# Layer 1's attention: how far ahead the maximum pass runs

## The reference

```
Q, K, V = x @ W_Q.T, x @ W_K.T, x @ W_V.T        # split into 16 heads of 8
attn  = einsum('bhqd,bhkd->bhqk', Q, K) / sqrt(8)
attn  = where(tril(ones((1024, 1024))), attn, -inf)
probs = softmax(attn, axis=-1)
y     = einsum('bhqk,bhkd->bhqd', probs, V)
return y @ W_O.T
```

## Time and profile before

| what | us |
|---|---|
| median of three runs (1268.46 to 1277.15) | 1268.52 |
| profiled execution | 1278.86 |
| its span | 1276.6 |
| TensorE busy | 1111.2 (87%) |
| VectorE busy | 801.0 (63%) |
| ScalarE busy | 647.2 (51%) |
| GpSimd busy | 193.5 (15%) |
| mean granted clock of TensorE, share of full speed | 0.900 |

### The profile page before, as it was taken

How to read it: one execution, slowest core, us unless ns; L and a number is a source line. 1 busy time by engine, 2 the same in 40 slices (tenths; PEclk the granted TensorE clock), 3 DMA queues, 4 the chain that set the end, 5 groups by cost and what they waited for, 6 DMA issues and landing times.

```text
span 1276.6 us, 19532 instructions
## 1 busy us (share of the span) xinstructions
PE 1111.2 (87%) x7306; PEld 521.5 (41%) x7306; DVE 801.0 (63%) x1582; ACT 647.2 (51%) x1246; POOL 193.5 (15%) x312
## 2 busy tenths in 40 slices
PE   6499999699999999999854799899999899897777
PEld 4366666222222222222222344344442567553344
DVE  6633333498898899887047687788870435455654
ACT  4323322137787777778524156567775322424344
POOL 2145554000011010010100001112321000001000
PEclk9799999759999999999877589889995699899888
DMA  4612223311112101100004302211223300000331
GB/s 122 205 48 88 91 90 73 92 26 36 44 48 60 49 20 35 45 11 19 10 10 143 132 28 79 78 45 47 86 86 93 105 3 1 1 1 0 133 133 33
DMA packets 62551, 78.06 MB, mean 61 GB/s; under 512 B 16046, under 2 KB 40318, under 8 KB 60414
## 3 DMA queue, kind: packets, MB, share of 16 engines
q1 hardware_dynamic: 53962, 66.67, 17.0%
q10 hardware_dynamic: 8500, 10.21, 2.8%
HBM read 61.58 MB, written 14.62 MB: 60 GB/s over the span
## 4 chain that ended last, share of the span: by engine, by line
PE 64%; DVE 18%; ACT 7%; DMA 4%; SPq 4%; issue 2%; ACTq 0%; POOL 0%; DVEq 0%
PE PS L1543 62%; DVE mx L1336 10%; ACT arena L899 5%; SPq L558 2%; DMA arena<-k_dram 1%; SPq L566 1%; DMA arena<-drev_dram 1%; PE PS L1556 1%; DVE arena L1150 1%; DVE arena L1517 1%; SPq L577 0%; DVE arena L1153 0%; DMA arena<-mrow 0%; PE PS L1911 0%; DMA fw<-sum_dram 0%
## 5 line engine op out<-in xcount | busy, mean ns | idle before, releaser
L1543 PE MATMUL PS<-arena 128*32 128x512 f32 (+13 forms) x3656 | 618.1, 491 | 62.4 <-ACT arena L899 16.1
L1336 DVE TENSOR_REDUCE mx<-PS 128x1 f32<-128x512 f32 (+3 forms) x896 | 500.7, 623 | 103.0 <-PE PS L1543 102.2
L899 ACT ACTIVATE arena<-PS 128x512 f32<-128x512 f32 (+3 forms) x896 | 436.5, 556 | 241.7 <-PE PS L1543 234.1
L1543 PEld LDWEIGHTS PS<-arena 128*32 128x32 f32 (+3 forms) x3656 | 159.9, 105 | 439.0 <-DVE mx L1336 163.4
L1543 PE MATMUL PS<-x_hi,w_hi_lo 128*128 128x512 f32 x320 | 145.1, 495 | 0.8 <-DVE combT L1214 0.4
L1435 DVE TENSOR_TENSOR fw<-PS,fw 128x512 f32<-128x512 f32 x80 | 55.3, 691 | 119.8 <-ACT fw L946 118.0
L946 ACT ACTIVATE fw<-PS 128x512 f32<-128x512 f32 x80 | 47.8, 597 | 123.5 <-PE PS L1543 123.5
L831 POOL TENSOR_TENSOR fw<-fw,arena 128x512 f32<-128x512 f32 x64 | 84.9, 1326 | 88.9 <-DVE fw L1435 88.9
L1543 PE MATMUL PS<-fw 128*128 128x512 f32 (+3 forms) x184 | 90.7, 580 | 0.0
L784 POOL TENSOR_TENSOR arena<-arena,fw 128x512 f32<-128x512 f32 x32 | 40.7, 1272 | 297.4 <-DMA fw<-sum_dram 297.4
L1543 PEld LDWEIGHTS PS<-x_hi,w_hi_lo 128*128 128x128 f32 x320 | 61.2, 191 | 31.1 <-issue 19.4
(11 more groups left out here) (288 smaller groups left out, 1070.6 us busy)
## 6 DMA issues: line engine op xcount, KB each, us to landing
arena<-comb_dram SPq DMA_DIRECT2D x16, 1024.0 KB, 5.1
fw<-sum_dram SPq DMA_DIRECT2D x32, 256.0 KB
arena<-comb_dram SPq DMA_DIRECT2D x16, 512.0 KB, 7.7
q_dram<-arena SPq DMA_DIRECT2D x24, 256.0 KB, 3.8
k_dram<-arena SPq DMA_DIRECT2D x24, 256.0 KB, 3.7
arena<-drev_dram SPq DMA_DIRECT2D x32, 192.0 KB, 4.2
arena<-k_dram ACTq DMA_DIRECT2D x20, 204.0 KB
fw<-in_ffn_w SPq DMA_DIRECT2D x10, 384.0 KB, 3.1
```

The costliest lines, as they stand in the source:

```text
L899: s.activation(Pr[:, m % 8, 0:w], bank(4 + m % 3, 0, w), ACT.Exp).then_inc(A["e_done"], 1)
L1336: v.reduce_max(mx[:, H % 2, kh, n:n + 1], bank(U % RING, 0, w), axis=AX.X, negate=True).then_inc(A["ring_free"], 1)
L1543: return nc.tensor.matmul(out_, lhsT, rhs, start=start, stop=stop)
```

## The change

Two values change. `LAG[1]` goes from 2 to 1: in layer 1, slot H of SP's and GpSimd's loops now handles the maximum of half H+1 and not of half H+2. And the mark of half H (other than half 0) is `ends[H] + 24` in place of `ends[min(H + 1, HALVES - 1)] + 8`. Layer 0 is not touched, and no instruction is added or removed.

```diff
-LAG = (1, 2)
+LAG = (1, 1)
 COMBINE_AFTER, MAX_AFTER = 1, (8, 5)
 GATE_HALF, COMB_HALF = 4, 7
 PROJECT = 5
@@ def stands_before(layer, H, ends):
     if layer == 0:
         return ends[H] + 20
-    return ends[0] + 14 if H == 0 else ends[min(H + 1, HALVES - 1)] + 8
+    return ends[0] + 14 if H == 0 else ends[H] + 24
```

## The result

The changed kernel takes 1432.63 us (median of four runs, 1423.15 to 1435.48) against 1272.2 us of the kernel before in the same comparison: a ratio of 1.124 (95% interval 1.119 to 1.129; it is taken over all runs and is not the quotient of the two medians). That is 160 us more. I had said 1402, with a range of 1350 to 1465. Its profiled execution took 1435.14 us, with a span of 1432.9.

A forecast was written before the change was run, and what follows sets the result against it. TensorE was taken to set the pace, VectorE close behind. The terms 5.4 + 78.5 + 4.2 + 21 + 24 - 4.2 - 2.7 + 7.4 = +133.6 on the median of 1268.52 gave 1402 us, range 1350 to 1465.

The forecast's parts named there:

- The rows at an even-to-odd border and M behind them: Six borders: TensorE waits for the maximum's rows, then GpSimd's parts for M: +78.5 us, and +4.2 before VectorE works again.
- The odd-to-even border: Rows need 7.4 us and 4.4 are left after the reciprocal: 3 us of stall, seven times, +21 us.
- The half us by which VectorE trails: At odd-to-even borders, about half a us added to the rows' 7.4 us because VectorE trails.
- Half 15's rows: Half 14's border has no M behind it, so it costs only the rows' wait: +7.4 us.
- The clock: 8 us at half speed after each of six even-to-odd stalls, so 4 lost each: +24 us.
- The marks: Moved units: six pairs of halves 2 to 13 +5.4 us, half 1 -4.2, half 14 at full clock -2.7.
- 0.25 us: TensorE time of one unit, from an odd half's 20.6 us with 32 units and 12.65 without.
- 16.0 us by VectorE: Length of an even half with 32 units, from VectorE's share of 13.8 to 15.6 us plus copies and reciprocal.
- the stall alone: Rival: only the even-to-odd stall costs, clock back at once, odd-to-even rows covered: 1357 us, 16%.
- Half clock throughout the odd halves: Rival: clock loss of 16.6 us in place of 4 in six odd halves, hiding 18 of 21: 1460 us, 22%.
- Not slower: Rival: at even-to-odd borders the rows arrive in time and parts precede normalise, so no stall: 1252 us, 2%.

The follow-up runs named there:

- Runs 2 to 5: The changed kernel with, in order, the rows ahead of the sums (1407.0 us), the parts ahead (1406.86), both ahead (1310.54), or the reciprocal earlier (1310.18).
- run 2: The changed kernel with layer 1's SP issuing the maximum's rows of half H+1 before it waits for the reciprocal: 1407.0 us, ratio 1.1062.
- run 3: The changed kernel with GpSimd making two halves' parts in even slots, ahead of normalise, SP's order as changed: 1406.86 us, ratio 1.1078.
- Run 10: The changed kernel with needless f32 matmuls filling TensorE's whole wait, ahead of the rows and of M, in halves 3, 5, ..., 13: 1417.85 us, ratio 1.1119.
- run 11: The kernel before with needless matmuls ending each step of halves 14 and 15: three bf16 ones, 1268.44 us, or one f32, 1266.13 us.
- run 1: The new marks alone, with the old LAG of 2, timed beside the kernel before: 1311.94 us, ratio 1.0315.
- Run 7: New marks with LAG 2, each unit of layer 1's maximum pass cut to its first 128 columns: 1264.63 us, ratio 0.9873 to the kernel before.
- run 8: The changed kernel with 40 needless 48-row matmuls of 512 columns ahead of the wait for the rows in halves 3, 5, ..., 13: 1421.18 us, ratio 1.1188.
- run 5: The changed kernel with VectorE's reciprocal behind step 0 of an even half and step 2 of an odd one: 1310.18 us, ratio 1.0313.

## Why the prediction was right, and where it was not

The direction, the range and the mechanism of the stalls held; the size of two terms didn't. That 1433 lay in the range and 30 us from the forecast is in part luck: the clock was taken 12 us too large, and the marks 42 too small. Step by step, with the terms of the sum:

- **The rows at an even-to-odd border and M behind them**, 78.5 + 4.2: measured 67.2 + 13.2 = 80.4 us. Runs 2 to 5 show that both hang on the reciprocal at the end of an even half, and that each alone holds the half for a like time: the parts 85.5 us (run 2), the rows 66.4 at these six borders (run 3).
- **The odd-to-even border**, 21: measured 20.9 over seven. They are 1.6 to 6.7 us each, where I had 3. One reading was off: the 2.03 us to land begin at 722.89 with the issue of the fourth DMA and not behind it, so 3.04 + 2.03 counts 0.7 us twice. And the landing was longer here, 2.5 to 5.75 us from that point, longest at the border where TensorE waits 6.7. That the sum agrees is in part luck. The half us by which VectorE trails was not tested by itself.
- **Half 15's rows**, 7.4: measured 7.8.
- **The clock**, 24, taken between bounds of 12 and 100 (six borders at 2 and at 16.6): too large. Run 10 gives 12.2 us for the six borders. By difference, the changed kernel less the marks alone is 120.7 us, of which 109.1 are waits; 11.6 remain, within runs that spread by more than 10. I had weighed halves 14 and 15 too much: in half 9, with its 17 units, the clock was back after some 6 us. The first bound, 2 us a border, was the nearer one. The Trainium skill (TensorE: Matmul & The Clock Gate, "What's actually happening") would have the ramp at less than 1% of the span, here under 14.3 us. For what the stalls add that agrees, with 12.2 us in run 10. With half 15, which that sentence may not mean, it doesn't: 25.4 us here at 0.50 against 16.8 at 1.00 in run 11 are another 8.6.
- **The marks**, 5.4 - 4.2 - 2.7 = -1.5: measured +41 (run 1). This is the term that was mis-sized most, and two of its steps failed. (Its counts of 32 and 16 units, and of 12 in half 14, are off by one or two: the plan has 31, 17 and 10. The columns are right.)

The first is "without units an odd half takes 25.3 us at 1.2 GHz, so 12.65 at 2.4". Not all of those 25.3 us run with TensorE's clock. The changed kernel's chain in half 15, at 0.50 as before:

```profile
1135.15 0.59 ACT arena L899
1135.74 0.05 issue
1135.79 3.05 PE PS L1543 x11
1138.84 0.59 ACT arena L899
```

Of 3.69 us a step, 3.05 are TensorE's and would halve; the exponential stays. With eight of those (4.7 us) kept, 25.3 becomes (25.3 - 4.7) / 2 + 4.7 = 15.0, and with run 11's fillers in it half 15 took 16.8. So a unit was not worth 0.25 us either: 15 units fewer made half 9 only 1.2 us shorter (19.44 to 18.27, run 1), and TensorE's idle time in it grew from 0.35 to 1.46 us. Taking units out opens the pause for that exponential again. I had 16.6; in run 1 an odd half takes 18.3 to 19.2 us where the clock is 1.00 throughout and 19.1 on average, 2.5 too little in each of six, 15 us. Half 1, from copy to copy, takes 22.5 there for 16.6 (5.9 more), and half 14 takes 14.3 for 8.8 (5.5 more).

The second is the even half, 16.0 us by VectorE. From first exponential to first exponential it takes 18.25 on average, 2.25 more in each of six, 13.5 us. VectorE's share was about right (14.95 us in half 8), but it alone doesn't set the length: TensorE is busy for 17.81 of the 18.60 us, because its clock is at 0.50 in the middle of the half. It falls behind the first step:

```profile
888.00:890.00 2.00, 1.81 (x18) 1.15 (x18) 2.00 (x4) 1.26 (x4) 0.00 (x0) 1.00 0.12 45
890.00:892.00 2.00, 1.83 (x12) 0.84 (x10) 2.00 (x6) 0.39 (x1) 0.89 (x5) 0.72 0.00 0
892.00:894.00 2.00, 2.00 (x11) 0.28 (x9) 0.82 (x2) 0.49 (x1) 1.92 (x3) 0.50 0.04 8
```

Run 7, where these halves take 9.9 us at 1.00, supports the width of the units as the cause. Whether the clock falls because TensorE is held back by VectorE's reductions, which are without a gap just before, or because so many of its matmuls there are over 48 rows, as run 8's fillers are, no run separates. With these, the marks come to -1.5 + 15 + 13.5 + 5.9 + 5.5 = 38 of the 41 us.

Of the rivals, the stall alone (1357) had the clock right and the marks and borders wrong. Half clock throughout the odd halves (1460) was as close in the number as the forecast, for a wrong reason: the odd halves have a mean clock of about 0.8, and the missing time lay in the marks. "Not slower" had its point right: with the reciprocal early (run 5) the stalls are gone. But its price counted on the same wrong odd half; what is left is 1310 and not 1252.

What stays open is what decides whether TensorE's clock holds, in the even halves of run 1, in half 15 (at 0.50 in the changed kernel, at 0.72 in run 3) and under the fillers of run 8. No run isolates it.

## What to carry to other kernels

When work that is needed one stage ahead shares an in-order queue with a wait from the end of the present stage, its lead is gone, whatever the loop's look-ahead says; look for everything that waits on that one event and mend all of it, since mending one of two waits of like length gave only a fifth here. A stage's time at half clock is not twice its time at full clock: take the other engines' links of the chain out first. And a stage whose engine is "95% busy" can still be bound by a chain, in which case moving work out of it gives little back (1.2 us for 15 units), while the stage that gets the work pays in full. And when a change moves work between stages, cut the windows at the stages' own ends: cut at the copies, both kinds of half seemed to hold what neither did.

## What the runs showed of the hardware

TensorE's granted clock fell to 0.50 while it was busy without a gap, under 40 bf16 matmuls over 48 of 128 rows (1014 to 1020 us of run 8), and was at 1.00 behind a wait filled with f32 matmuls over 128 rows (run 10). With three of the narrow kind a step halves 14 and 15 were at 1.00, where the same halves without them stay at 0.50 at 94% busy. From the start of the fourth issue the rows took 2.03 us to land in the kernel before and 2.5 to 5.75 us at the odd-to-even borders of the changed one.
